# The expert router of a LoRA-expert layer: its four column groups of the PE array split the tokens instead of the contraction, and VectorE turns the logits

## What is computed

```
xc     = x[b] @ w_cond[id[b]].T                    # 1024 x 1024, one of 8 matrices by id
logits = xc @ W_router.T                           # 8 experts
probs  = softmax(logits); keep the top 2, renormalized -> combine (8 per token)
h      = einsum('nd,erd->ner', xc, A_stack)        # 8 experts x rank 16 = 128 rows
lora   = einsum('ner,eor->no', h * combine, B_stack) * 2.0
out    = x + xc @ W_base.T + b_base + lora
```

## Time and profile before

| | us |
|---|---|
| median of three runs | 403.37 |
| the profiled execution | 402.67 |
| its span, first to last instruction | 400.9 |
| TensorE busy | 394.9 (99%) |
| VectorE busy | 302.2 (75%) |
| ScalarE busy | 185.6 (46%) |
| mean granted TensorE clock | 1.00 of full speed |

### The profile page before, as it was taken

The page is one execution under the profiler, slowest core; times in us unless marked ns, Lnnn a source line. Parts: engine busy times, 40 slices in busy tenths (PEclk is TensorE's granted clock), DMA queues, the critical chain, the costliest instruction groups (busy, mean ns, idle before and its releaser), DMA issues.

```text
span 400.9 us, 5336 instructions
## 1 busy us (share of the span) xinstructions
PE 394.9 (99%) x2008; PEld 329.7 (82%) x2008; DVE 302.2 (75%) x430; ACT 185.6 (46%) x285; POOL 39.9 (10%) x67
## 2 busy tenths in 40 slices
PE   8999999999999999999999999999999999999996
PEld 7888878888788888888888887888886888888885
DVE  3898957789799999864547697668868999987311
ACT  4886743748633345222145776257656233441000
POOL 0101100101000040021172000000000003001110
PEclk9999999999999999999999999999999999999999
DMA  7998881768430056375669868256083003532222
GB/s 234 363 348 308 300 334 37 256 232 294 152 105 2 27 183 207 135 263 209 201 220 370 316 230 296 76 165 219 37 275 139 6 12 109 195 108 78 79 80 78
DMA packets 21226, 72.94 MB, mean 182 GB/s; under 512 B 2832, under 2 KB 2848, under 8 KB 21200
## 3 DMA queue, kind: packets, MB, share of 16 engines
q1 hardware_dynamic: 15984, 56.11, 40.3%
q0 software_dynamic: 4928, 15.97, 11.4%
q10 hardware_dynamic: 288, 0.52, 0.4%
HBM read 64.20 MB, written 8.39 MB: 181 GB/s over the span
## 4 chain that ended last, share of the span: by engine, by line
PE 97%; DMA 1%; SPq 1%; ACT 0%; DVE 0%; issue 0%
PE bank_x L786 29%; PE bank_x L790 15%; PE bank_y L771 9%; PE bank_y L773 9%; PE bank_y L772 9%; PE bank_x L771 8%; PE bank_x L772 8%; PE bank_x L773 8%; PE bank_y L830 2%; DMA raw<-x 1%; PE bank_y L848 0%; PE bank_y L856 0%; SPq L353 0%; ACT x_hl L484 0%; SPq L337 0%; DVE out_sb L581 0%
## 5 line engine op out<-in xcount | busy, mean ns | idle before, releaser
L786 PE MATMUL bank_x<-x_hl,wc_hl 128*128 128x512 f32 x512 | 128.9, 393 | 1.5 <-ACT wc_hl L484 1.5
L530 DVE TENSOR_TENSOR wc_hl<-raw,wc_hl 128x1024 fp32r<-128x1024 f32 x90 | 108.8, 1221 | 22.1 <-ACT wc_hl L462 22.1
L462 ACT CAST wc_hl<-raw 128x1024 fp32r<-128x1024 f32 x90 | 93.9, 1050 | 65.8 <-PE bank_y L773 35.0
L786 PEld LDWEIGHTS bank_x<-x_hl,wc_hl 128*128 128x128 f32 x512 | 92.1, 189 | 18.4 <-ACT wc_hl L484 1.9
L790 PEld LDWEIGHTS bank_x<-x_hl,wc_hl 128*128 128x128 f32 x512 | 70.1, 190 | 5.2
L790 PE MATMUL bank_x<-x_hl,wc_hl 128*128 128x256 f32 x512 | 71.7, 282 | 0.0
L414 POOL DMA_DIRECT2D out<-out_sb x28 | 15.3, 545 | 254.0 <-DVE out_sb L581 232.2
L573 DVE SCALAR_TENSOR_TENSOR out_sb<-bank_x,bias_sb,out_sb 128x512 f32<-128x512 f32 x32 | 23.8, 748 | 22.2 <-PE bank_x L773 16.6
L772 PE MATMUL bank_x<-x_hl,wc_hl 128*128 128x512 f32 x96 | 37.4, 390 | 0.0
L771 PE MATMUL bank_x<-x_hl,wc_hl 128*128 128x512 f32 x96 | 37.4, 390 | 0.0
L773 PE MATMUL bank_x<-x_hl,wc_hl 128*128 128x512 f32 x96 | 37.4, 389 | 0.0
(11 more groups left out here) (89 smaller groups left out, 483.8 us busy)
## 6 DMA issues: line engine op xcount, KB each, us to landing
raw<-w_cond SPq DMA_DIRECT2D x62, 512.0 KB, 4.9
raw<-w_base SPq DMA_DIRECT2D x24, 512.0 KB, 5.2
out_sb<-x POOLq DMA_DIRECT2D x32, 256.0 KB, 5.2
raw<-x SPq DMA_DIRECT2D x15, 512.0 KB, 4.9
out<-out_sb POOLq DMA_DIRECT2D x28, 256.0 KB, 2.3
raw<-w_cond SPq DMA_DIRECT2D x4, 256.0 KB, 4.4
out<-out_sb SPq DMA_DIRECT2D x4, 256.0 KB, 2.0
raw<-x ACTq DMA_DIRECT2D x2, 256.0 KB, 2.7
```

What stands on the lines that cost most here:

```text
L462: nc.scalar.copy(split_dst(key, HI), split_src(key)).then_inc(hi_done, 1)
L530: nc.vector.tensor_tensor(split_dst(key, LO), split_src(key), split_dst(key, HI).bitcast(F32), ALU.subtract).then_inc(lo_done, 1)
L786: nc.tensor.matmul(ps[:], wc_hl[:, slot_of(s, t), HI, k], x_hl[:, s % 2, k].rearrange("p h n -> p (h n)"), start=(k == 0), stop=False)
```

## The change

The router now runs all 8 k steps in each column group, each group over its own 128 of the 512 tokens: 32 products of 128 columns instead of 8 of 512. `ps_logit` then has the finished logits of tokens 128j + c on partitions 32j to 32j+31 and in columns c from 0 to 127. VectorE's transpose of 32 x 32 blocks, straight from PSUM, gives token on partition and expert on the free axis. ScalarE's copy, TensorE's four transposes and VectorE's sum over parts are gone. The order of tokens in `gate_er` differs from that in `h_sb`, so the product in `gate_h` reads and writes in permuted views.

```diff
@@ make_gate (VectorE)
-                dve.wait_ge(tok_done, p + 1)
-                chain(nc.vector.tensor_reduce(logit[:], tok_parts, AX.X, ALU.add))
+                dve.wait_ge(router_done, p + 1)
+                chain(nc.vector.transpose(logit_sb[:].rearrange("p q n -> p (q n)"), ps_logit[:, 0:P]))
@@ gate_h (VectorE)
-                nc.vector.tensor_tensor(h_sb[:], h_sb[:], ps_tok[:], ALU.mult).then_inc(h_gated, 1)
+                h_of = h_sb[:].rearrange("p (j b n) -> p j b n", j=CG, b=NQ)
+                gate_of = ps_tok[:].rearrange("p (b j n) -> p j b n", b=NQ, j=CG)
+                nc.vector.tensor_tensor(h_of, h_of, gate_of, ALU.mult).then_inc(h_gated, 1)
@@ ScalarE
-            def copy_logits(p):
-                act.wait_ge(router_done, p + 1)
-                nc.scalar.copy(logit_t, ps_logit[:]).then_inc(logit_copied, 1)
@@ router (TensorE)
-                    j = k % CG
-                    mm = nc.tensor.matmul(ps_logit[j * NR:(j + 1) * NR, :], wr_sb[:, k], xp[:, p % 2, k],
-                                          start=k < CG, stop=k >= CG, tile_position=(0, j * NR))
+                    for j in range(CG):
+                        mm = nc.tensor.matmul(ps_logit[j * NR:(j + 1) * NR, 0:P], wr_sb[:, k],
+                                              xp[:, p % 2, k, j * P:(j + 1) * P],
+                                              start=(k == 0), stop=(k == KT - 1), tile_position=(0, j * NR))
@@ lora_down (TensorE)
-                    if k == HT:
-                        pe.wait_ge(logit_copied, p + 1)
-                        if p == 0:
-                            pe.wait_ge(consts_in, 16)
-                    if k == HT:
-                        for q in range(NQ):
-                            tok = nc.tensor.transpose(ps_tok[:, q * P:(q + 1) * P], logit_t[:, q * P:(q + 1) * P],
-                                                      ident)
-                        tok.then_inc(tok_done, 1)
@@ gate_to_rows (TensorE)
+                if p == 0:
+                    pe.wait_ge(consts_in, 16)
@@ wait_bank, stage P2, first bank (TensorE)
-                    pe.wait_ge(logit_copied, 2 * g + 2)
+                    pe.wait_ge(gate_ready, 2 * g + 2)
```

More of the change, by code:

```diff
@@ L225, in build @@
         gate_er = sb("gate_er", [P, NQ, EXPERTS, RANK])
-        logit_t = gate_er[:].rearrange("p q e r -> p (q e r)")
-        logit = sb("logit", [P, NQ, EXPERTS])
+        logit_sb = sb("logit_sb", [P, NQ, NR])
+        logit = logit_sb[:, :, 0:EXPERTS]
         shifted = sb("shifted", [P, NQ, EXPERTS])
@@ L243, in build @@
         ps_logit, ps_h, ps_tok = bank_y[0], bank_y[1], bank_y[3]
-        tok_parts = ps_tok[:].rearrange("p (q j n) -> p q n j", q=NQ, j=CG)[:, :, 0:EXPERTS]
         consts_in = sem("consts_in")
@@ L262, in build @@
         router_done = sem("router_done")
-        logit_copied = sem("logit_copied")
-        tok_done = sem("tok_done")
         gate_step = sem("gate_step")
@@ L507, in _ @@
                     if s % GSEQS == 1:
-                        copy_logits(2 * g)
                         exp_and_h(2 * g)
@@ L512, in _ @@
                     hi(key)
-                copy_logits(2 * g + 1)
                 for key in stages["window"][2:]:
@@ L607, in make_gate @@
                 v4 = [P, NQ, EXPERTS, EXPERTS]
-                dve.wait_ge(tok_done, p + 1)
-                chain(nc.vector.tensor_reduce(logit[:], tok_parts, AX.X, ALU.add))
+                dve.wait_ge(router_done, p + 1)
+                chain(nc.vector.transpose(logit_sb[:].rearrange("p q n -> p (q n)"), ps_logit[:, 0:P]))
                 ready()
-                chain(nc.vector.tensor_reduce(mx, logit[:], AX.X, ALU.max))
+                chain(nc.vector.tensor_reduce(mx, logit, AX.X, ALU.max))
                 ready()
-                chain(nc.vector.tensor_tensor(shifted[:], logit[:], per_token(mx), ALU.subtract))
+                chain(nc.vector.tensor_tensor(shifted[:], logit, per_token(mx), ALU.subtract))
                 dve.wait_ge(exp_done, p + 1)
```

## The result

The changed kernel takes 399.84 us (median of five runs, 399.32 to 400.54) where the kernel before takes 403.28 (five runs beside it, 403.09 to 404.32): ratio 0.9919, 95% interval 0.9900 to 0.9937. Timed twice more on other occasions it gave 399.85 us, 0.9912 (0.9889 to 0.9934), and 400.00 us, 0.9927 (0.9911 to 0.9944). The medians differ by 3.44, 3.17 and 2.88 us. The forecast was 400.5 us in 399.3 to 403.7, 2.9 us faster.

A forecast was written before the change was run, and what follows sets the result against it. The prediction took TensorE's stream as the bound: 4 x (0.29 router + 0.44 transposes) = 2.9 us less, putting the median at 400.5 us. Its own range was 399.4 to 401.6, for 8 in 10 399.3 to 403.7.

The forecast's parts named there:

- The bound: Whole kernel: time is the sum of what TensorE streams; time saved on ScalarE or VectorE alone is worth nothing.
- The router, 0.29 forecast: Each router falls from 2.16 to 1.87 us because a stall goes, saving 0.29 us, 1.2 us over four.
- the 0.30: Old router: stall of the fourth column group, whose product k = 7 waits 0.30 us for VectorE's line 671.
- The price of a narrow pass: Router: a 128-column pass beside three others costs 0.108 us, so 16 passes per group take 1.73 us.
- the burst of starts: Old router: eight loads fall into 0.16 us, column groups starting some 7 ns apart, so the four run side by side.
- The rule of starting in program order: Rival at the router's 32 products: narrow passes don't overtake, 3.70 us per router, 407.8 us in all; chance 0.08.
- The transposes, 0.44 forecast: Line 848 between router and next conditional step: removing four float32 transposes saves 0.44 us per pair, 1.8 us in all.
- What is late next is nothing: Router: k = 0 to 6 run until 54.41, the k = 7 operand is ready at 54.03, so 0.38 us are spare.
- a sign against itself: Router, line 823: the forecast expected no records held back for VectorE's sum (line 664).
- Gates, copies, the lead before cond(3, 3): ScalarE and VectorE changes stay hidden; ScalarE's 0.86 us lead before cond(3, 3) covers 0.73 us; cost none.
- some 4 us earlier: Pair 0's gate chain on VectorE no longer waits for the transposes, so it comes some 4 us earlier.
- The range: Whole kernel: own range 399.4 to 401.6 us, from router saving 0 to 0.38 and 0.5 us of scatter.

## Why the prediction was right

- **The bound.** That the time is TensorE's stream was right: putting 0.47 and 0.26 us per pair back into it gave 2.07 and 0.99 us of time, and 5.0 us of work put back on VectorE with 3.1 on ScalarE gave nothing.
- **The router, 0.29 forecast.** Right in size and cause. 1.88 us stand against 1.87, and the old router without its late operand lost the 0.30. With the products behind it the gain is 0.26 to 0.28.
- **The price of a narrow pass.** 0.108 taken, 0.109 measured, alone as four abreast. The argument from the burst of starts was good for the order that the change uses, and only for it: the prediction said that the engine lets a group's first pass go ahead. It does so until a group has four passes handed out. With two passes of a group in a row, as here, all groups fill evenly, and holding the rest back costs nothing (1.88 us).
- **The rule of starting in program order.** The Trainium skill ("TensorE: Matmul & The Clock Gate", "The mechanism") would have made the router 3.7 us by the forecast's sum. The trace disagrees: starts overtake across column groups. The Trainium skill's 81 ns for a matmul of 128 columns with its load (same page, "Back-to-back issue gap") fits neither a group alone (109 ns in float32, or 2.04 cycles of 2.4 GHz a column) nor four abreast (1.88 us / 64 = 29 ns).
- **The transposes, 0.44 forecast.** Put back they cost 0.47. Of what pair 0 gained, 0.72 - 0.28 = 0.44 is theirs; in the odd pairs it is 0.48. The sum of the traces is 2.95 us, where the forecast's terms give 4 x 0.73 = 2.92.
- **"What is late next is nothing".** True for the executions without a late load; the step is too sure. In the first profile of the changed kernel the 0.38 us of spare time were used up and 0.61 more, and 8 records were held back for VectorE's sum, which the prediction had named as a sign against itself; one other profile shows the same. In the two undisturbed profiles only 0.18 and 0.12 us were spare (1.51 less 1.33 and 1.39). The spare time was measured against one execution of a chain that begins with a DMA.
- **Gates, copies, the lead before cond(3, 3).** No wait of TensorE appears at any of these places in the changed kernel. But "some 4 us earlier" for the gate chain was too much. Its first instruction came 1.5 us earlier in the first profile (57.75 for 59.25) and 2.45 in the second (56.80). The router was done at 54.87 there, and a weight split (line 521, 55.66 to 56.89) stood ahead of it in VectorE's stream, which the forecast left out. It cost nothing, as the gates have cover.
- **The range.** The forecast's own 399.4 to 401.6 does not follow from its terms: a router saving of 0 gives 401.6 and one of 0.38 gives 400.1, and half a microsecond of scatter makes that 399.6 to 402.1. All three medians lie in either.
- **What the sum leaves.** 3.44, 3.17 and 2.88 us between the medians against 2.95 in the traces. Each interval holds 2.95, but two of three medians lie above it. Whether a few tenths are real stays open. One candidate was not tried: the wide router wants its last operand 0.88 us behind its start (53.78 - 52.90) and the narrow one 1.51, so an execution with a late load may cost the kernel before more.

## What to carry to other kernels

When an operand comes late, split the work by output rather than by contraction step, so that every parallel unit has all its early work before it needs the late piece: the stream was no shorter than before, and losing the stall was worth 0.26 us a router. With its operand ready the wide form was 0.07 us better than the narrow one, so the split pays only against a late operand. When small products run side by side in column groups, alternate the groups in the instruction stream; how many of one group stand in a row decides, and it falls off a cliff (1.88, 1.96, 4.26, 5.89 us for 2, 4, 8, 16 passes in a row). A price missing from the trace can be taken from two different rows that agree (here the wide pass divided by four, and the transposes), if the bounds stay in the range.

## What the runs showed of the hardware

- A float32 pass of 128 columns takes 0.109 us with 32 weight columns, alone or beside three others. A pass of 8 columns with 128 float32 weight columns takes 0.114 us, and the Trainium skill ("TensorE: Matmul & The Clock Gate", "LDWEIGHTS (loading the stationary operand)") gives the number of weight columns over 1.2 as ns for a load, 107 for these: the trace's pace lies 7% above it.
- Each column group appears to hold four passes, and the fifth for a full group stops the others. Forecast from this, the order with eight in a row came out at 4.26 against 4.15 us.
- The first full-array product behind a router takes 0.43 us in the chain where its fellows take 0.23, wherever the router stands: with the router behind `lora_down` the eight products of the next conditional step took 2.04 us instead of 1.84, and the first of `lora_down` took 0.23.
- In the router with passes of 8 columns the granted clock went from 1.00 to 0.50 while TensorE was shown as busy for 4.60 of 4.60 and 4.80 of 4.80 us. No other kernel of this study had a mean clock under 0.99.
